# A buffer of its own for the attention's normalised rows, and four expert-output buffers in place of six, in a fused feed-forward/attention/feed-forward kernel

## What is computed

```python
x = x + 0.5 * ffn(layernorm(x))      # ffn 0
x = x + attn(layernorm(x))
x = x + 0.5 * ffn(layernorm(x))      # ffn 1

def ffn(x):                          # 16 experts, 4 chosen per token, and 2 shared ones
    g = einsum('th,eih->tei', x, gate_w); u = einsum('th,eih->tei', x, up_w)
    yo = einsum('tei,ehi->teh', silu(g) * u, down_w)
    return einsum('te,teh->th', combine, yo) + silu(x @ sh_gate.T) * (x @ sh_up.T) @ sh_down.T

def attn(x):                         # linear attention, 16 heads of 16
    q = softplus(gelu(x @ q_w1.T + q_b1) @ q_w2.T + q_b2);  k = the same with k_*
    v = gelu(x @ v_w.T + v_b);  g = gelu(x @ g_w.T + g_b)
    z = 1 / (einsum('bhcn,bhc->bhn', q, k.sum(-1)) * SCALE + dim)
    out = einsum('bhnm,bhdm->bhdn', einsum('bhcn,bhcm->bhnm', q, k), v) * SCALE
    return ((out + v) * z * g) @ p_w.T + p_b
```

## Time and profile before

| what | value |
|---|---|
| time of 3 runs | median 1819.06 us (1814.09 to 1829.95) |
| the profiled execution | 1810.68 us |
| its span, first to last instruction | 1808.6 us |
| mean granted TensorE clock | 0.970 of full speed |
| PE busy | 1649.0 us, 91% |
| ACT, DVE, POOL busy | 49%, 61%, 58% |

### The profile page before, as it was taken

The page is one execution under the profiler, slowest core; times in us unless marked ns, Lnnn a source line. Parts: engine busy times, 40 slices in busy tenths (PEclk is TensorE's granted clock), DMA queues, the critical chain, the costliest instruction groups (busy, mean ns, idle before and its releaser), DMA issues.

```text
span 1808.6 us, 39999 instructions
## 1 busy us (share of the span) xinstructions
PE 1649.0 (91%) x12493; PEld 1264.2 (70%) x12493; DVE 1099.8 (61%) x3414; ACT 893.7 (49%) x1376; POOL 1041.6 (58%) x1186
## 2 busy tenths in 40 slices
PE   5757999889989999999999999899999989989998
PEld 4535777677767777787777787577777767867655
DVE  4786457664854456457556655557556576744775
ACT  6323445336565665465656656536656545433111
POOL 3477765777772337733464464363566767763760
PEclk9878999999999999999999999999999999999999
DMA  9547999799855659884765677474688889999440
GB/s 299 191 143 191 242 254 236 231 251 233 233 162 121 161 147 247 229 198 120 165 175 146 151 199 174 110 175 119 167 211 203 213 219 249 239 255 232 146 134 24
DMA packets 502897, 343.39 MB, mean 190 GB/s; under 512 B 333591, under 2 KB 471982, under 8 KB 502702
## 3 DMA queue, kind: packets, MB, share of 16 engines
q1 hardware_dynamic: 456434, 214.92, 48.7%
q0 software_dynamic: 46080, 125.89, 25.3%
q10 hardware_dynamic: 188, 0.03, 0.0%
HBM read 96.37 MB, written 168.82 MB: 147 GB/s over the span
## 4 chain that ended last, share of the span: by engine, by line
PE 41%; POOL 26%; issue 11%; DVE 10%; SPq 5%; DMA 5%; ACT 2%; DVEq 0%; POOLq 0%; ACTq 0%
POOL yg L1487 13%; POOL xd L1473 11%; PE bank L1135 7%; PE bank L988 5%; PE bank L990 4%; PE bank L989 4%; PE bank L1188 4%; SPq L962 3%; PE bank L1139 3%; DMA yg<-yd,idx 2%; PE bank L1078 2%; PE bank L1079 2%; PE bank L1083 2%; DVE xb L1766 2%; PE bank L1150 2%
## 5 line engine op out<-in xcount | busy, mean ns | idle before, releaser
L1473 POOL DMA_INDIRECT xd<-xs,idx x480 | 483.5, 1007 | 429.1 <-DVE picked L1627 221.9
L1487 POOL DMA_INDIRECT yg<-yd,idx x480 | 474.7, 989 | 178.5 <-issue 142.8
L988 PE MATMUL bank<-xtp,gu_hi 128*128 128x128 f16 (+1 forms) x1728 | 369.8, 240 | 26.2 <-DMA xtp<-xd 10.3
L989 PE MATMUL bank<-xtp,gu_hi 128*128 128x128 f16 (+1 forms) x1728 | 368.7, 239 | 0.0
L990 PE MATMUL bank<-xtp,gu_lo 128*128 128x128 f16 (+1 forms) x1728 | 367.8, 239 | 0.0
L1135 PE MATMUL bank<-dn,h 128*128 x1152 | 310.6, 393 | 30.3 <-DVE h L1727 16.8
L1342 ACT ACTIVATE ybuf<-bank 128x512 f32<-128x512 f32 x288 | 171.2, 595 | 295.2 <-PE bank L1135 262.5
L1727 DVE SCALAR_TENSOR_TENSOR h<-bank,h 128x512 f32<-128x512 f32 x240 | 165.5, 690 | 226.6 <-PE bank L990 146.1
L1335 ACT ACTIVATE h<-bank 128x512 f32<-128x512 f32 x240 | 141.9, 596 | 307.1 <-PE bank L1083 181.1
L1135 PEld LDWEIGHTS bank<-dn,h 128*128 128x128 f32 x1152 | 206.6, 193 | 72.5 <-issue 43.8
L1766 DVE SCALAR_TENSOR_TENSOR xb<-yg,comb,xb 128x256 f32<-128x256 f32 x480 | 195.3, 479 | 93.6 <-DMA yg<-yd,idx 93.6
(11 more groups left out here) (239 smaller groups left out, 2778.7 us busy)
## 6 DMA issues: line engine op xcount, KB each, us to landing
yd<-ybuf SPq DMA_DIRECT2D x144, 256.0 KB
yd<-ybuf SPq DMA_DIRECT2D x288, 128.0 KB
xr<-xb SPq DMA_DIRECT2D x30, 512.0 KB
xb<-xr SPq DMA_DIRECT2D x30, 512.0 KB, 5.1
xb<-in_attn_x_dram SPq DMA_DIRECT2D x16, 512.0 KB, 5.8
out_dram<-xb SPq DMA_DIRECT2D x16, 512.0 KB
xd<-xs,idx POOLq DMA_INDIRECT x480
yg<-yd,idx POOLq DMA_INDIRECT x480
```

What stands on the lines that cost most here:

```text
L988: pe.matmul(out_ap, a_hi, b_hi, start=(i == 0), stop=False)
L989: pe.matmul(out_ap, a_hi, b_lo, start=False, stop=False)
L1473: pool.indirect_dma_start(out=xd[buffer_of[q]][:, :], out_offset=bass.IndirectOffsetOnAxis(ap=idx[:, r % SEQS, t, k:k + 1], axis=0), in_=x ...
L1487: pool.indirect_dma_start(out=yg[:, half, t % 2, j].bitcast(U32), out_offset=None, in_=yd[buffer_of[q]][:, :], in_offset=bass.IndirectOffs ...
```

## The change

`xna` becomes an SBUF tile of its own, 4 KB a partition. `normA(n)` then waits only for `turnA(n-1)`, the reader of the same tile, instead of `kv(n-1)` (and, for n = 0, no longer for the last weight, whose staging lies in `kqx`); `add_bias` loses its wait for `turnA`. To make room `RING_Y` goes from 6 to 4, 2 KB a partition each, so `yev(t)` waits for the store of tile t - 4.

```diff
-RING_Y = 6
+RING_Y = 4
...
-        piece("normA", n, ("rootA", n), ("kv", n - 1) if was else ("turn_w", self.n_weights - 1))
+        piece("normA", n, ("rootA", n), *[("turnA", n - 1)] * was)
         piece("turnA", n, ("normA", n), *[("gproj", (n - 1, 1))] * was)
...
-        xna = kqx[:, 0]
+        xna = sb("xna", [P, TT, D])
...
             def normA(n):
                 if n:
-                    act.wait_ge(kv_done, n)
-                else:
-                    act.wait_ge(w_turned, len(groups))
+                    act.wait_ge(turnedA, 2 * n)
                 normalise(0, n, stay_of(SEQS + n), xna).then_inc(xna_done, 1)
...
                 else:
                     dve.wait_ge(kv_done, n)
-                dve.wait_ge(turnedA, 2 * n + 2)
                 for b in range(2):
```

## The result

The changed kernel took 1872.96 us in the median of 3 runs (1859.59 to 1876.48), against 1819.06 before: a ratio of 1.0276 with a 95% interval of 1.0205 to 1.0348. It is 54 us slower. The forecast was 1832, with a range up to 1860.

A forecast was written before the change was run, and what follows sets the result against it. PE was taken to bound the kernel, so only its idle time could change. Terms -5 (norm's buffer) +2 (table loads) +16 (four buffers) = +13 us: 1823.7 profiled, 1832 as median; range 1804 to 1860.

The forecast's parts named there:

- What bounds the kernel: Whole kernel: PE bounds it, its work is unchanged by the edit, and time can fall only by PE's idle time.
- Part 1: Attention stretch: normA no longer waits for kv; PE's direct waits for second and kv go, -5 us (bounds -29 to 0).
- The rival in which the overlap pays 29 us: Attention stretch: ACT's waiting starves the expert units, half of PE's idle time goes; -27 us in sum, 1792; chance 0.08.
- Part 2: ACT's list: 17 more table loads, 21.8 us of ACT, of which +2 us reach the end (bounds 0 and 21.8).
- its rival: ACT's list: the table loads all land on the path, +22 in place of +2; sum +33 us, 1852; chance 0.05.
- Part 3: Evictions into ybuf: with four buffers they wait for late stores behind SP's transposing loads; +16 us (bounds 0 and 36.7).
- Once per stage: Stages where SP lags: one late eviction in each of four, since PE is then behind and SP catches up; 36.7 us.
- one delay serves several evictions: Stages where SP lags: SP's total work is unchanged and it catches up while PE waits; argued against the full 36.7 us.
- The second rival, the ring in full: First and last stage: late evictions fill the down bank and h; 36.7 in place of 16, sum +34 us, 1853; chance 0.20.
- Its sign: What would show the full ring cost: the first and last stage are each over 10 us longer.
- The three quarters for the deferred `down` pieces: PE's order: down behind more gates and ups gives PE other work during late evictions; 21.7 us cut to +16.
- The first rival (ring hidden): Evictions into ybuf: deferred down pieces and shared units cover the late ones; sum -3 us, 1816; chance 0.20.

## Why the prediction was wrong, point by point

**What bounds the kernel: right.** PE's instructions are the same, and the time came as idle time of PE (+42 us) and, for the rest, as longer busy time (+20.6) of the same instructions. The busy time was forecast to stay at 1649. The granted clock is 0.94 in place of 0.98 in the last stage, the stage in which PE stands still most often. What part of the 20.6 us is the clock's was not measured by itself.

**Part 1, the norm's own buffer, -5 us: not borne out, and not refuted.** With its order it measured 0.0%, within 0.24% either way, or 4 us, just short of the term. ACT's wait for `kv` went, and POOL's `shift` took half its place. Of PE's waits, the 5.4 us that the term was read from did go: in the run with six buffers `second` and `kv` wait 0.0. But `apply` waits 5.1 us there in place of 0.4, and 12.6 in the changed kernel, and the term had no such wait. The rival in which the overlap pays 29 us got no support: the own buffer with six costs and gives nothing. It is not refuted outright, because the own buffer always came with a new order, and other new orders cost 18 to 41 us; the own buffer at the old order was not tried.

**Part 2, table loads, +2 us: nothing speaks against it, much against its rival.** 26 more loads, nine more than in the changed kernel, stood in a run that took as long as before; all on the path they would have cost 26 x 1.283 = 33 us, and something else in that order would have had to give 33 us back. Load and drain together, 2.66 us a switch by the Trainium skill ("ScalarE: Activation LUTs", What ACT_TABLE_LOAD costs), would have made an estimated 26 x 2.66 = 69 us of ACT's time. The trace agrees with the load, 1283 ns each; no idle time of the drain's size stands ahead of the loads (1.1 us ahead of 61 of them in the same run).

**Part 3, four buffers, +16 us: this step failed, in the count of the late evictions.** The mechanism was right and was seen: late stores behind SP's transposing loads, PE held at `down` by the one bank. The term measured 39 us at an unchanged order. I had counted one late eviction in each of four stages, 36.7 us in all. At the unchanged order ACT's waits for stores grew by 90.1 us, from 20.8 in 7 times to 110.9 in 30: in the first stage by 33.6 where I had 10.4, in the last by 26.5 where I had 11.4, in the second and third by 12.0 and 11.3 where I had 8.4 and 6.5, and by 6.6 in the fifth, where I had nothing. "Once per stage" and "one delay serves several evictions" were the wrong premises: the waits came again and again in the same stage, as SP's timeline has new transposing loads ahead of the stores of each pair. The share that reaches PE was not far off: PE's waits for evictions grew by 53.8 - 12.3 = 41.5 us, 0.46 of the 90.1, where I had 0.59, and 41.5 is about the 39 measured.

The second rival, the ring in full, had the right size for this term, 36.7, and I gave it 0.20. That it fits is chance: it passes one lateness per stage on whole, and what happened is that about half of two and a half times as much was passed on. Its sign, the first and the last stage each over 10 us longer, was met at the unchanged order (12.5 and 14.3) and not in the changed kernel (0.5 and 0.0). There the waits for stores are also not mostly in these two stages: 42.2 of the 89.6 us.

**The three quarters for the deferred `down` pieces: right as a discount, but the price of the order was left out.** With the own buffer the step from six to four buffers costs 37 us at the order made for six and 54 - 26 = 28 at the one made for four, 0.76 of it; with `kqx` shared 39 and 49 - 41 = 8. In the first stage of the changed kernel ACT waits 9.4 us for stores, in place of 37.3 at the old order. So the new order does help against the late stores. But it is not free: with six buffers, so that it had nothing to help against, it cost 41 us without the own buffer and 26 with it.

**What the sum had no term for.** This is the second step that failed: I priced the new order by its table loads alone, +2 us, and it is half of the loss. Two small changes of the planner's numbers, with nothing else changed, cost 18 and 28 us; the order with the own buffer and six planned cost 0. So the new orders of this kernel's lists that were tried cost anything from 0 to 41 us. Of the changed kernel's 54 us, 22 to 27 go when only the ring is made longer at its own order, and 26 to 28 stay with the order. Why each of these orders is slower was not tried piece by piece, and stays open. Of the 26 with the own buffer, `apply` can be a part: with six buffers on the chip PE waits 13.0 us for DVE's `mix` there, where it waited 0.4 before. The order made for four without the own buffer, run with six, shows PE waiting longer for loaded rows and for DVE's product in the groups by line, here for the gate's first matmul:

```profile
L989 PE MATMUL bank<-xtp,gu_hi 128*128 128x128 f16 (+1 forms) x1728 | 377.4, 243 | 55.3 <-DMA xtp<-xd 22.4 <-DVE h L1728 21.7 <-issue 10.1
```

against this line before:

```profile
L988 PE MATMUL bank<-xtp,gu_hi 128*128 128x128 f16 (+1 forms) x1728 | 369.8, 240 | 26.2 <-DMA xtp<-xd 10.3 <-issue 9.5 <-DVE h L1727 5.7
```

**The first rival (ring hidden): refuted.** I had also read it out of the rule to double-buffer in the Trainium skill ("Trainium Kernel Development and Optimization", Best Practices). The rule names no number for a ring like this one, and as one it doesn't hold here: at one order four buffers take 1.024 and five 1.006 of the time with six, and eight are no better (0.998). What counts is how long a buffer is held, and in the case of rows 6 and 7 18 of its 23 us are the wait of its store for the issuer.

## What to carry to other kernels

The number of buffers that a ring like this one needs is set by how long one is held, from its filling to the landing of its store; read it in the timelines of the filler and the issuer, since the store can stand in the issuer's list for longer than it flies. When such a ring is shortened, price every late hand-over and not one per stage, and then take the share that reaches the bottleneck from rows (here about half). And when a planner makes the order, run one or two neighbours of the old order as a control: the old order can be a lucky one, as it was here, and what a change costs by reordering can be as large as what it costs by itself.

## What the runs showed that I had not expected

Moving 432 stores from SP's list to ACT's freed the ring and still made the kernel some 52 us slower. ACT's issues take 351 and 389 ns in the middle, as the view of `ybuf` shows, 432 of them some 157 us, on an engine that was 49% busy before, and it waited some 40 us more for its own evictions:

```profile
L1348 ACTq DMA_DIRECT2D yd<-ybuf x288: 338/351/1937, 184.2 to 1747.9; - x144
L1350 ACTq DMA_DIRECT2D yd<-ybuf x144: 378/389/466, 169.1 to 1737.1; - x144
```

The same run shows PE waiting three times as long for loaded rows although SP had fewer issues to make. Whether the transposing loads and the stores disturb each other once they come from two issuers was not tried by itself.

The two costs of four buffers, waits and order, hide each other for the most part when `kqx` is shared (49 where 80 would be the sum), and less with the own buffer (54 where 37 + 26 = 63 would be). What the changed kernel lost is so about one half late stores and one half order.
